# Graph attention over edges: scores as two full-array matmuls on block keys, and keys copied one item ahead

## The chip, the core and the metric

The kernel runs on one core of a Trainium2 chip. The metric is the device time of one execution in microseconds (us). The kernel before was run three times: 1605.08, 1602.91 and 1599.86 us, median 1602.91. The trace and the profile's page below come from one further execution, taken by the hardware profiler.

## The reference, cut to what matters

A graph of 6250 nodes with 256 features has 106,250 edges. After a layer norm, each node sends its row to its neighbours with attention weights, and the result is added to the input. A mixture-of-experts layer (8 experts, top 2) follows; the change does not touch it.

```
q = tanh(x @ Wq + bq)                     # 6250 x 25
k = x @ Wk + bk                           # 6250 x 25
w = sum(q[src] * k[dst]) / 5              # one score per edge
alpha = softmax of w over the edges of one dst
out = segment_sum(alpha * x[src], dst)    # 6250 x 256
x = x + out
x = x + moe(layernorm(x))                 # top-2 of 8 experts, 256 -> 512 -> 256
```

## The kernel before, in words

There are three stages. The first normalises the rows, computes q and k and writes a table of rows (256 features, a one, 25 values of q) to memory. The second is the edge loop. The third runs the experts.

The edge loop handles 106 items. An item has two halves (called x), each a group of 512 edges (four sub-groups j of 128) and a window of 64 target nodes. So 128 partitions hold the nodes of both halves. For an item *a* the engines do this, each with its own written order:

- **GpSimd (POOL)** issues eight indirect gathers of 128 rows each into one of four slots of `xg` (`gather`, line 586). The gathers for item a wait until the sums of item a-4 are done (semaphore `s_pv`).
- **ScalarE (ACT)** runs `item` (lines 1409 to 1416): it copies q out of the slot once the gathers have landed (line 1392), takes the exponentials of item a-1 (lines 1401 and 1402), copies the keys of item a (four copies, one for each 32 nodes, line 1386), copies the transposed q (line 1397), and copies the transposed probabilities of item a-1 (line 1407).
- **TensorE (PE)** runs `item` (lines 1660 to 1666): two transposes of q (line 1631), four transposes of the probabilities of a-1 (line 1647), the scores of a (line 1640), the weighted sums of a-1 (line 1655). The scores are eight matmuls with 25 rows, 64 columns of weights and 128 moving columns, for two halves and four sub-groups, into four PSUM banks. The sums are eight matmuls with 64 columns of weights and 257 moving columns.
- **VectorE (DVE)** copies the running maxima (line 931), subtracts, masks and reduces the scores of item a (line 936), stores the maxima (line 943), makes the mask of item a+1 (line 921), and adds the sums of a-1 to the accumulator (line 954).

Four items form a `quad`; the loop over quads runs with values read from a table at run time, so the windows and groups are computed in registers (lines 322 and 332). Six times in the loop a chunk of 896 nodes is complete. In such a quad VectorE also normalises the finished rows (`finished`, lines 988 to 1013), and in the next one it sorts them to experts (`route`, lines 1048 to 1120); ScalarE and TensorE have their share in both. The SyncE queue loads indices and targets for each item; at the end of the loop it waits until the keys of the last item have been copied (semaphore `s_kts`) and then issues the loads of the first experts' weights (lines 474, 475 and 480), which overwrite the keys' memory.

Of the kernel before, what the change touches and what calls it, by code (L numbers as in the profile page):

```python
# [28 lines left out]
P = 128  # L29
N = 6250  # L30
D = 256
S = 25
# [13 lines left out]
HP = P // 2  # L46
# [7 lines left out]
G = 4  # L54
# [5 lines left out]
BAND = P // G  # L60
ROW = D + 1 + S
W1COLS = D + 1
# [15 lines left out]
DK = 5.0  # L78
# [18 lines left out]
def build(nc, x, src, dst, Wq, bq, Wk, bk, gamma, beta, Wr, br, W1, b1, W2, b2, out):  # L97
    ctx = ExitStack()
    with ctx:
        def sb(name, shape, dt=F32):  # L100
            return ctx.enter_context(nc.sbuf_tensor(name, shape, dt))
# [17 lines left out]
        ident = sb("ident", [P, P])  # L119
# [7 lines left out]
        wqk = sb("wqk", [P, 2, 2 * S])  # L127
        bqk = sb("bqk", [P, 2 * S])
        bkcol = sb("bkcol", [P, 1])
# [27 lines left out]
        done_i = arena_b[0:1, 9788:9789].bitcast(I32)  # L157
        done_b = arena_b[0:1, 9789:9789 + NE]
        gidx_e = arena_b[:, 9797:9797 + 2 * EARLY].bitcast(I32)


        arena_a = sb("arena_a", [P, 12712])
        qz = arena_a[:, 0:NT * S].rearrange("p (t s) -> p t s", t=NT)
        rawf = arena_a[:, 1300:1300 + 1024]
# [58 lines left out]
        idx = sb("idx", [P, XSLOTS, 2, G], I32)  # L223
        kts = sb("kts", [P, P])
        qs = sb("qs", [P, 2, G, BAND])
        qT = sb("qT", [P, 2, P])
# [31 lines left out]
        wsel = sb("wsel", [P, 2])  # L258
        weq = sb("weq", [P, 2])
        wtok = sb("wtok", [P, 2])  # L260
        tokB = sb("tokB", [P, 2], I32)
        b1e = sb("b1e", [P, 4])
        gidx = sb("gidx", [P, 2], I32)
# [3 lines left out]

        score_banks = ps[:, 4 * 512:8 * 512].rearrange("p (j n) -> p j n", j=G)[:, :, 0:P]
        sums_bank = [pb[3], pb[1]]
# [407 lines left out]
        def _(v):  # L677
# [17 lines left out]
            v.memset(ltok[:, :], 0.0).then_inc(s_v0, 1)  # L695
            v.memset(kT[:, NT * P:NTX * P], 0.0).then_inc(s_v0, 1)
            v.sem_inc(s_acc, 2)
            v.sem_inc(s_mask, PEEL)
# [75 lines left out]
            def group_lists():  # L774

                v.wait_ge(s_grpb, 1)
                for b in range(2):
                    v.tensor_copy(cntb[:, 2 * b:2 * b + 2, :].rearrange("p k (q h) -> p k h q", h=2),
                                  pb[6 + b][:, 0:4 * GP].rearrange("p (k h q) -> p k h q", k=2, h=2)).then_inc(s_grpd, 1)
                v.wait_ge(s_v0, 16)  # L780
                v.wait_ge(s_grpd, 10)
# [105 lines left out]
            v.wait_ge(s_kc, 1)  # L887
            v.wait_ge(s_v0, 16)
            v.tensor_copy(segf[:, 0:NCH - 1], pb[7][0:1, 0:NCH - 1]).then_inc(s_sg, 1)
# [35 lines left out]
            def maximum(b, tiles, a, number, first=False):  # L925

                if not first:
                    v.wait_ge(s_ms, number(a))
                    v.sem_inc(tk_v, 1)
                for r in range(4):  # L930
                    ins = v.tensor_copy(nmo[quarters[r], b:b + 1], nm_all[quarters[r], bass.ds(tiles(r // 2, a)[r % 2], 1)])  # L931
                ins.then_inc(s_om, 1)
                v.wait_ge(s_om, number(a + 1))
                v.wait_ge(s_sc, number(a + 1))
                v.sem_inc(tk_v, 1)
                v.tensor_tensor_reduce(out=sc[:, b, :].rearrange("p (j n) -> p j n", j=G), in0=score_banks[:, :, :],  # L936
                                       in1=mask[:, b, :].rearrange("p (j n) -> p j n", j=G), scale=-1.0 / DK,
                                       scalar=nmo[:, b:b + 1], op0=ALU.add, op1=ALU.min,
                                       accum_out=nbias[:, b:b + 1]).then_inc(s_nb, 1)
                v.wait_ge(s_nb, number(a + 1))  # L940
                v.sem_inc(tk_v, 1)
                for r in range(4):
                    ins = v.tensor_copy(nm_all[quarters[r], bass.ds(tiles(r // 2, a)[r % 2], 1)], nbias[quarters[r], b:b + 1])  # L943
                ins.then_inc(s_ms, 1)
# [335 lines left out]
        def _(a):  # L1280
# [5 lines left out]
            for o, i in ((bqk[:, 0:S], bq.partition_broadcast(P)),  # L1286
# [5 lines left out]
                a.dma_start(o, i).then_inc(s_wl, 16)  # L1292
            a.wait_ge(s_v0, 16)
            for j in range(G):
# [87 lines left out]

            def copy_keys_of(tiles, a_):
                for r in range(4):
                    cols = slice(r * BLK, (r + 1) * BLK)
                    ins = nc.scalar.copy(kts[:, cols], kT3[:, bass.ds(tiles(r // 2, a_)[r % 2], 1), cols].rearrange("p o n -> p (o n)"))
                ins.then_inc(s_kts, 1)

            def copy_q(s, landed):
                a.wait_ge(s_g[s], landed)  # L1390
                a.sem_inc(tk_a, 1)
                nc.scalar.copy(qs[:, :, :, 0:S], xg[:, s * 2 * G:(s + 1) * 2 * G, W1COLS:ROW]  # L1392
                               .rearrange("p (x j) d -> p x j d", x=2)).then_inc(s_qs, 1)
# [11 lines left out]
            def copy_probs(b, done):  # L1405
                a.wait_ge(s_pt, done)
                nc.scalar.copy(probT[:, b, :], pb[2][:, :]).then_inc(s_pts, 1)

            def item(tiles, a_, number, landed, between=None):
                copy_q(a_ % XSLOTS, landed)  # L1410
                exponentials((a_ - 1) % 2, number(a_))
                copy_keys_of(tiles, a_)
                copy_qT(number(a_ + 1))
                copy_probs((a_ - 1) % 2, number(a_))
                if between is not None:
                    between()

            number = counter(a, 0)
            copy_keys_of(tiles, 0)
            copy_q(0, 32 * G)  # L1420
            copy_qT(1)
            item(tiles, 1, number, 32 * G)
            def quad(k, ends=None, routes=None):

# [123 lines left out]
        def _(pe):  # L1548
# [79 lines left out]
            def q_transposes(done):  # L1628
                pe.wait_ge(s_qs, done)
                for x_ in range(2):  # L1630
                    last = nc.tensor.transpose(pb[0][:, x_ * P:(x_ + 1) * P], qs[:, x_, :, :].rearrange("p j s -> p (j s)"), ident[:, :])  # L1631
                last.then_inc(s_qt, 1)

            def scores(done):
                pe.wait_ge(s_kts, done)
                pe.wait_ge(s_qTs, done)
                for x_ in range(2):
                    for j in range(G):
                        band = slice(j * BAND, j * BAND + S)
                        last = mm(score_banks[HP * x_:HP * x_ + HP, j, :], kts[band, HP * x_:HP * x_ + HP], qT[band, x_, :],  # L1640
                                  start=True, stop=True)
                last.then_inc(s_sc, 1)
# [17 lines left out]
            def item(a, number, between=None):  # L1660
                q_transposes(number(a + 1))
                prob_transposes((a - 1) % 2, number(a))
                scores(number(a + 1))
                sums((a - 1) % 2, (a - 1) % XSLOTS, number(a), number(a))
                if between is not None:
                    between()
# [8 lines left out]
            q_transposes(1)  # L1675
            scores(1)
            item(1, number)
# [170 lines left out]
```

## Time and profile before

| | |
|---|---|
| median of three runs | 1602.91 us |
| profiled execution, span from first to last instruction | 1973.1 us |
| edge loop in the profiled execution, first to last gather | 94.36 to 1538.11 us |
| TensorE busy | 57% of the span |
| GpSimd busy | 56% |
| VectorE busy | 43% |
| ScalarE busy | 25% |
| granted TensorE clock, mean over the span | 0.700 |

The page gives no other time for the profiled execution than its span, and the span is 370 us longer than the median of the runs. Busy shares are means over stages of very different kind: the first stage, the edge loop and the experts. A time at the start of a row of the timeline is counted from the first instruction, the next number is how long the work took, and the square brackets say how long the engine had been idle and who ended it.

### The profile page before, as it was taken

The numbers are of one execution on the slowest core, as the hardware profiler recorded it, in microseconds if no ns is written. First come the engines' busy times: TensorE is split into PE (matmuls) and PEld (weight loads), VectorE is DVE, ScalarE is ACT, GpSimd is POOL, SyncE is SP. The second block draws the span as 40 slices with busy tenths as digits, with TensorE's granted clock in tenths as the row PEclk, the third lists the DMA queues.
The fourth block names the chain that finished last, engine by engine and source line by source line (L and its number), as shares of the span: only waits on it lengthen the run. The fifth ranks groups of instructions, "written<-read, shape, count | busy, mean of one in ns | idle before, by whom it ended". The sixth has DMA issues, their size and how long they took to land.

```text
span 1973.1 us, 30781 instructions
## 1 busy us (share of the span) xinstructions
PE 1132.6 (57%) x6718; PEld 766.9 (39%) x6719; DVE 840.2 (43%) x3273; ACT 499.6 (25%) x1477; POOL 1114.7 (56%) x1111
## 2 busy tenths in 40 slices
PE   6623444444445445455354445454454789999997
PEld 6511222322223223122232223122231568888886
DVE  7513343454344534444345334444445653333332
ACT  3511122121212122122121222122121433443342
POOL 3255666464665565646644664646654357677676
PEclk9756666565656556666565666666565799999999
DMA  8554434344333534533435333534345435554554
GB/s 185 135 114 106 107 101 104 105 112 107 103 104 106 128 102 111 127 97 102 105 88 123 101 102 94 130 93 105 101 112 125 131 72 95 91 106 81 94 94 64
DMA packets 155658, 210.22 MB, mean 107 GB/s; under 512 B 59526, under 2 KB 122462, under 8 KB 155431
## 3 DMA queue, kind: packets, MB, share of 16 engines
q0 software_dynamic: 61360, 151.84, 32.4%
q1 hardware_dynamic: 74921, 40.52, 8.6%
q10 hardware_dynamic: 19278, 16.96, 3.6%
q14 instruction: 87, 0.70, 0.1%
q8 instruction: 12, 0.20, 0.0%
HBM read 174.36 MB, written 34.41 MB: 106 GB/s over the span
## 4 chain that ended last, share of the span: by engine, by line
PE 23%; issue 23%; DVE 19%; another core or an unknown queue 16%; DVEq 12%; SPq 2%; ACT 2%; ACTq 1%; DMA 1%; POOL 0%; POOLq 0%
PE pb L1766 8%; PE pb L1775 8%; DVEq L332 5%; DVE acc L954 3%; DVE arena_b L936 3%; DVEq L322 3%; DVE nmo L931 2%; DVE nm_all L943 2%; PE pb L1756 1%; PE pb L1655 1%; PE pb L1707 1%; DVE ab L1111 1%; DVEq L954 1%; DVE mask L921 1%
## 5 line engine op out<-in xcount | busy, mean ns | idle before, releaser
L586 POOL DMA_INDIRECT arena_a<-rows_dram,idx x848 | 813.8, 960 | 652.4 <-issue 240.2
L1655 PE MATMUL pb<-arena_a,arena_b 128*64 128x257 f32 x1696 | 358.1, 596 | 8.1 <-issue 4.5
L954 DVE SCALAR_TENSOR_TENSOR acc<-acc,alpha,pb 32x257 f32 x424 | 203.4, 480 | 319.8 <-issue 175.8
L1640 PE MATMUL pb<-qT,kts 25*64 25x128 f32 x1696 | 75.6, 425 | 340.8 <-ACT qT L1397 331.7
L1647 PE MATMUL pb<-ident,arena_b 128*128 128x128 f32 x424 | 94.7, 363 | 251.5 <-ACT arena_b L1401 158.9
L1655 PEld LDWEIGHTS pb<-arena_a,arena_b 128*64 128x64 f32 x1696 | 171.7, 211 | 155.8 <-issue 119.1
L1401 ACT ACTIVATE arena_b<-arena_b,nbias 128x512 f32<-128x512 f32 x106 | 76.4, 721 | 549.4 <-DVE nbias L936 407.5
L1766 PE MATMUL pb<-arena_a,arena_b 128*128 128x256 f32 x832 | 192.0, 384 | 1.2 <-ACT arena_a L1503 1.2
L630 POOL DMA_INDIRECT out_dram<-arena_a,tokB x104 | 166.1, 1597 | 45.2 <-issue 26.0
L1775 PE MATMUL pb<-arena_b,arena_a 128*128 128x256 f32 x832 | 188.3, 379 | 0.6 <-DVE arena_a L1177 0.6
L1640 PEld LDWEIGHTS pb<-qT,kts 25*64 25x64 f32 x1696 | 37.3, 192 | 370.6 <-issue 346.6
L1647 PEld LDWEIGHTS pb<-ident,arena_b 128*128 128x128 f32 x424 | 64.5, 186 | 277.9 <-ACT arena_b L1401 174.9
L1766 PEld LDWEIGHTS pb<-arena_a,arena_b 128*128 128x128 f32 x832 | 159.9, 193 | 23.9 <-issue 1.4
L1775 PEld LDWEIGHTS pb<-arena_b,arena_a 128*128 128x128 f32 x832 | 154.1, 190 | 19.7 <-DVE arena_a L1177 0.9
L1514 ACT ACTIVATE arena_a<-pb,b1e 128x256 f32<-128x256 f32 x208 | 98.7, 474 | 220.5 <-PE pb L1766 191.3
L936 DVE CUSTOM_DVE_ANT_0 arena_b<-pb,mask,nmo 128x512 f32<-128x512 f32 x106 | 79.6, 751 | 175.1 <-remote 119.7
L609 POOL DMA_INDIRECT arena_a<-xn_dram,gidx x100 | 99.7, 997 | 65.3 <-PE pb L1756 45.0
L1177 DVE TENSOR_TENSOR arena_a<-pb,arena_b 128x256 f32<-128x256 f32 x104 | 43.9, 424 | 203.5 <-PE pb L1775 108.1
L921 DVE TENSOR_SCALAR mask<-arena_b,win_node 64x512 bf16<-64x512 int16 x214 | 79.1, 369 | 87.8 <-issue 79.1
L1397 ACT COPY qT<-pb 128x256 f32<-128x256 f32 x106 | 39.1, 369 | 279.2 <-remote 273.7
L931 DVE COPY nmo<-nm_all 32x1 f32 x424 | 61.4, 145 | 101.8 <-issue 95.2
L1631 PE MATMUL pb<-ident,qs 128*128 128x128 f32 x212 | 60.4, 378 | 45.9 <-ACT qs L1392 25.6
(236 smaller groups left out, 1231.2 us busy)
## 6 DMA issues: line engine op xcount, KB each, us to landing
arena_a<-rows_dram,idx POOLq DMA_INDIRECT x848
arena_b<-dst_dram SPq DMA_DIRECT2D x210, 64.0 KB
arena_b<-in_L_ffn_W_dram SPq DMA_DIRECT2D x16, 512.0 KB
rows_dram<-acc SPq DMA_DIRECT2D x12, 493.5 KB, 5.5
acc<-in_x_dram SPq DMA_DIRECT2D x13, 448.0 KB, 15.6
xn_dram<-arena_a ACTq DMA_DIRECT2D x6, 910.0 KB
out_dram<-arena_a ACTq DMA_DIRECT2D x12, 448.0 KB
idx<-srccol SPq DMA_DIRECT2D x214, 2.0 KB
```

The costliest lines, as they stand in the source:

```text
L586: g.indirect_dma_start(out=xg[:, (s * 2 + x_) * G + j, :], out_offset=None, in_=rows_dram[:, :], in_offset=bass.IndirectOffsetOnAxis(ap=id ...
L609: g.indirect_dma_start(out=xrows[:, k, :], out_offset=None, in_=xn_dram[0:rows_there, :], in_offset=bass.IndirectOffsetOnAxis(ap=columns[: ...
L630: g.indirect_dma_start(out=out[:, :], in_=ybuf[:, k, :], in_offset=None, out_offset=bass.IndirectOffsetOnAxis(ap=tokB[:, k:k + 1], axis=0) ...
L921: ins = v.tensor_scalar(mask[rows_of, b, :], dstb[rows_of, s, :], win_node[rows_of, bass.ds(window(x_, a), 1)], -BIG, ALU.not_equal, ALU.mult)
L931: ins = v.tensor_copy(nmo[quarters[r], b:b + 1], nm_all[quarters[r], bass.ds(tiles(r // 2, a)[r % 2], 1)])
L936: v.tensor_tensor_reduce(out=sc[:, b, :].rearrange("p (j n) -> p j n", j=G), in0=score_banks[:, :, :], in1=mask[:, b, :].rearrange("p (j n ...
L954: ins = v.scalar_tensor_tensor(out=mine, in0=mine, scalar=alpha[rows_of, b:b + 1], in1=sums_bank[b][rows_of, 0:W1COLS], op0=ALU.mult, op1= ...
L1640: last = mm(score_banks[HP * x_:HP * x_ + HP, j, :], kts[band, HP * x_:HP * x_ + HP], qT[band, x_, :], start=True, stop=True)
L1647: last = nc.tensor.transpose(pb[2][:, j * P:(j + 1) * P], sc[:, b, j * P:(j + 1) * P], ident[:, :])
L1655: last = mm(sums_bank[b][HP * x_:HP * x_ + HP, 0:W1COLS], probT[:, b, j * P + HP * x_:j * P + HP * x_ + HP], xg[:, (s * 2 + x_) * G + j, 0 ...
L1766: last = mm(banks[m][:, 0:ST], w1s[:, b, c, m * P:(m + 1) * P], xT[:, c, :], start=c == 0, stop=c == 1, skip_group_check=True)
L1775: last = mm(pb[3 + k2][:, 0:D], hT[:, c, k2 * P:(k2 + 1) * P], w2s[:, b, c, :], start=c == 0, stop=c == 3)
```

## The change

Line 1640's eight matmuls become two. The q of sub-groups 2h and 2h+1 of both halves are laid side by side before the transposes, so that one transposed tile has its 128 partitions filled with (sub-group parity o, half, feature). The keys are laid as blocks: for each parity o, the 64 columns of a half are non-zero only in the partitions of that half. One matmul for each o, 128 rows, 128 columns of weights and 256 moving columns, then gives the scores of two sub-groups for both halves. All scores now lie in one PSUM bank. The block keys take eight copies of 32 partitions by 32 columns in place of four of 128 by 32; they have two buffers, zeroed once at the start, and the keys of item a+1 are copied at the end of ScalarE's item a. VectorE's reduction reads one bank of 512 values in place of four pieces of 128. Some small tiles move into other memory, with no other instructions.

```diff
-        kts = sb("kts", [P, P])
-        qs = sb("qs", [P, 2, G, BAND])
+        kts = sb("kts", [P, 2, 2, P])
+        qs = sb("qs", [P, G, 2, BAND])
...
-        score_banks = ps[:, 4 * 512:8 * 512].rearrange("p (j n) -> p j n", j=G)[:, :, 0:P]
+        score_bank = pb[4]
+        score_pairs = score_bank[:, :].rearrange("p (h o n) -> p o h n", h=2, o=2)
...
+            v.memset(kts[:, :, :, :], 0.0).then_inc(s_v0, 1)
...
-                v.tensor_tensor_reduce(out=sc[:, b, :].rearrange("p (j n) -> p j n", j=G), in0=score_banks[:, :, :],
-                                       in1=mask[:, b, :].rearrange("p (j n) -> p j n", j=G), scale=-1.0 / DK,
+                v.tensor_tensor_reduce(out=sc[:, b, :], in0=score_bank[:, :], in1=mask[:, b, :], scale=-1.0 / DK,
...
-            def copy_keys_of(tiles, a_):
+            def copy_keys_of(b, tiles, a_):
                 for r in range(4):
                     cols = slice(r * BLK, (r + 1) * BLK)
-                    ins = nc.scalar.copy(kts[:, cols], kT3[:, bass.ds(tiles(r // 2, a_)[r % 2], 1), cols].rearrange("p o n -> p (o n)"))
+                    for o in range(2):
+                        band = slice((2 * o + r // 2) * BAND, (2 * o + r // 2 + 1) * BAND)
+                        ins = nc.scalar.copy(kts[band, b, o, cols],
+                                             kT3[band, bass.ds(tiles(r // 2, a_)[r % 2], 1), cols].rearrange("p o n -> p (o n)"))
                 ins.then_inc(s_kts, 1)
...
                 exponentials((a_ - 1) % 2, number(a_))
-                copy_keys_of(tiles, a_)
                 copy_qT(number(a_ + 1))
                 copy_probs((a_ - 1) % 2, number(a_))
+                copy_keys_of((a_ + 1) % 2, tiles, a_ + 1)
...
-            def scores(done):
+            def scores(b, done):
                 pe.wait_ge(s_kts, done)
                 pe.wait_ge(s_qTs, done)
-                for x_ in range(2):
-                    for j in range(G):
-                        band = slice(j * BAND, j * BAND + S)
-                        last = mm(score_banks[HP * x_:HP * x_ + HP, j, :], kts[band, HP * x_:HP * x_ + HP], qT[band, x_, :],
-                                  start=True, stop=True)
+                for o in range(2):
+                    last = mm(score_pairs[:, o, :, :], kts[:, b, o, :], qT[:, :, :], start=True, stop=True)
                 last.then_inc(s_sc, 1)
```

On ScalarE, in the second item of a quad, this stood from the exponentials to the transposed q (`kts` are the copied keys, `arena_b` holds the keys of all nodes, `qT` is the transposed q):

```order
L1402 ACTIVATE alpha<-nmo,nbias 128x1
L322 REGISTER_ALU x2
L322 ISA
L1386 COPY kts<-arena_b 128x32
L1386 ISA
...
L1397 COPY qT<-pb 128x256 [waits s_qt]
L1407 COPY arena_b<-pb 128x512 [waits s_pt]
L1437 REGISTER_ALU
L1392 COPY qs<-arena_a 128x8x25 [waits s_g0]
```

And this stands there now; the item's table word for the next keys is read here as well (`TENSOR_LOAD`):

```order
L1406 ACTIVATE alpha<-nmo,nbias 128x1
L370 REGISTER_ALU
L1401 COPY qT<-pb 128x256 [waits s_qt]
L1411 COPY arena_b<-pb 128x512 [waits s_pt]
L333 ISA
L333 TENSOR_LOAD item_row
L333 ISA x2
L323 REGISTER_ALU
L323 ISA
L1389 COPY kts<-arena_b 32x32
```

The copies of keys have moved from before the transposed q to behind the transposed probabilities, ahead of the wait for the next gathers.

On TensorE, the stretch of one item before was:

```order
L1631 MATMUL pb<-ident,qs 128x128 [waits s_qs]
L1631 MATMUL pb<-ident,qs 128x128
L1647 MATMUL pb<-ident,arena_b 128x128 [waits s_p]
L1647 MATMUL pb<-ident,arena_b 128x128 x3
L1640 MATMUL pb<-qT,kts 64x128 [waits s_qTs,s_kts]
L1640 MATMUL pb<-qT,kts 64x128 x7
L1655 MATMUL pb<-arena_a,arena_b 64x257 [waits s_acc,s_pts]
L1655 MATMUL pb<-arena_a,arena_b 64x257 x7
```

and is now, in the same place:

```order
L1650 MATMUL pb<-ident,arena_b 128x128 x3
L1644 MATMUL pb<-qT,kts 128x2x128 [waits s_qTs,s_kts]
L1644 MATMUL pb<-qT,kts 128x2x128
L1658 MATMUL pb<-arena_a,arena_b 64x257 [waits s_acc,s_pts]
L1658 MATMUL pb<-arena_a,arena_b 64x257 x7
```

The order of the steps is the same; eight matmuls of 64 by 128 columns have become two of 128 by 256.

## Rows read from the trace of the kernel before

**Rows 1.** The page: span, busy times, and the TensorE clock over 40 slices.

```profile
span 1973.1 us, 30781 instructions
PE 1132.6 (57%) x6718; PEld 766.9 (39%) x6719; DVE 840.2 (43%) x3273; ACT 499.6 (25%) x1477; POOL 1114.7 (56%) x1111
PEclk9756666565656556666565666666565799999999
```

**Rows 2.** By stretch: length; PE, PEld, DVE, ACT, POOL busy; clock; DMA share; GB/s.

```profile
0.00:110.00 110.00, 65.93 (x384) 59.18 (x385) 68.30 (x265) 44.01 (x119) 36.94 (x61) 0.84 0.71 158
110.00:1550.00 1440.00, 664.21 (x4374) 359.56 (x4374) 613.83 (x2298) 294.12 (x1017) 804.97 (x840) 0.61 0.42 107
1550.00:1973.00 423.00, 402.44 (x1960) 348.18 (x1960) 158.07 (x711) 161.50 (x341) 272.81 (x211) 0.98 0.48 92
```

**Rows 3.** The page's costliest groups: gathers.

```profile
L586 POOL DMA_INDIRECT arena_a<-rows_dram,idx x848 | 813.8, 960 | 652.4 <-issue 240.2
```

**Rows 4.** Timeline of GpSimd: the first gather of the loop, and the last.

```profile
94.36 1.07 POOL L586 DMA_INDIRECT arena_a<-rows_dram,idx  x1 [21.57 <-DMA rows_dram<-acc]
...
1538.11 0.96 POOL L586 DMA_INDIRECT arena_a<-rows_dram,idx  x1 [0.30 <-issue]
```

**Rows 5.** Timeline of all engines around one ordinary item.

```profile
616.19 1.96 PE L1655 MATMUL pb<-arena_a,arena_b 128*64 128x257 f32 x16
...
618.08 0.44 PE L1631 MATMUL pb<-ident,qs 128*128 128x128 f32 x2
...
622.29 1.11 PE L1647 MATMUL pb<-ident,arena_b 128*128 128x128 f32 x4 [3.77 <-ACT arena_b L1401]
...
625.11 0.37 ACT L1397 COPY qT<-pb 128x256 f32<-128x256 f32 x1 [1.35 <-remote]
...
625.26 1.96 DVE L954 SCALAR_TENSOR_TENSOR acc<-acc,alpha,pb 32x257 f32 x4 [1.25 <-remote]
...
625.82 0.96 POOL L586 DMA_INDIRECT arena_a<-rows_dram,idx  x1 [2.59 <-remote]
...
630.46 0.56 ACT L1386 COPY kts<-arena_b 128x32 f32 x4
...
638.10 0.95 POOL L586 DMA_INDIRECT arena_a<-rows_dram,idx  x1 [2.46 <-remote]
```

**Rows 6.** Timeline after a finished chunk: the first two items, and GpSimd.

```profile
386.85 0.37 ACT L1392 COPY qs<-arena_a 128x200 f32<-128x200 f32 x1 [1.53 <-issue]
...
390.74 0.34 ACT L1386 COPY kts<-arena_b 128x32 f32 x2 [1.39 <-issue]
...
391.50 0.74 PE L1640 MATMUL pb<-qT,kts 25*64 25x128 f32 x16 [2.44 <-ACT qT L1397]
...
392.16 3.70 PE L1655 MATMUL pb<-arena_a,arena_b 128*64 128x257 f32 x16
...
396.66 0.95 POOL L586 DMA_INDIRECT arena_a<-rows_dram,idx  x1 [14.00 <-PE pb L1655]
...
397.03 0.48 PE L1640 MATMUL pb<-qT,kts 25*64 25x128 f32 x16
```

**Rows 7.** VectorE's busy time while it finishes one chunk and sorts another.

```profile
585.06:600.00 14.94, 9.17 (x34) 0.50 0.40 103
...
651.97:676.10 24.13, 13.36 (x73) 0.50 0.74 173
```

**Rows 8.** The chain that ended last: transfers and matmuls after the loop.

```profile
1547.82 7.09 DMA arena_a<-xn_dram,arena_b
...
1592.56 2.81 DMA arena_a<-xn_dram,arena_b
...
1951.67 3.46 PE pb L1775 x16
```

**Rows 9.** Timeline of VectorE at the start: a memset, and the first statistics.

```profile
4.92 0.40 DVE L695 MEMSET ltok<- 128x408 f32 x1
...
8.96 2.38 DVE L706 BATCH_NORM_STATS2 st<-acc 128x6 f32<-128x256 f32 x7 [3.50 <-DMA acc<-in_x_dram]
```

More of the change, by code:

```diff
@@ L127, in build @@
         wqk = sb("wqk", [P, 2, 2 * S])
-        bqk = sb("bqk", [P, 2 * S])
         bkcol = sb("bkcol", [P, 1])
@@ L158, in build @@
         done_b = arena_b[0:1, 9789:9789 + NE]
+        b1e = arena_b[:, 9806:9810]
+        weq = arena_b[:, 9810:9812]
+        wtok = arena_b[:, 9812:9814]
         gidx_e = arena_b[:, 9797:9797 + 2 * EARLY].bitcast(I32)
         arena_a = sb("arena_a", [P, 12712])
+        bqk = arena_a[:, 9024:9024 + 2 * S]
         qz = arena_a[:, 0:NT * S].rearrange("p (t s) -> p t s", t=NT)
@@ L258, in build @@
         wsel = sb("wsel", [P, 2])
-        weq = sb("weq", [P, 2])
-        wtok = sb("wtok", [P, 2])
         tokB = sb("tokB", [P, 2], I32)
-        b1e = sb("b1e", [P, 4])
         gidx = sb("gidx", [P, 2], I32)
@@ L779, in group_lists @@
                                   pb[6 + b][:, 0:4 * GP].rearrange("p (k h q) -> p k h q", k=2, h=2)).then_inc(s_grpd, 1)
-                v.wait_ge(s_v0, 16)
+                v.wait_ge(s_v0, 17)
                 v.wait_ge(s_grpd, 10)
@@ L887, in _ @@
             v.wait_ge(s_kc, 1)
-            v.wait_ge(s_v0, 16)
+            v.wait_ge(s_v0, 17)
             v.tensor_copy(segf[:, 0:NCH - 1], pb[7][0:1, 0:NCH - 1]).then_inc(s_sg, 1)
@@ L1292, in _ @@
                 a.dma_start(o, i).then_inc(s_wl, 16)
-            a.wait_ge(s_v0, 16)
+            a.wait_ge(s_v0, 17)
             for j in range(G):
@@ L1391, in copy_q @@
                 a.sem_inc(tk_a, 1)
-                nc.scalar.copy(qs[:, :, :, 0:S], xg[:, s * 2 * G:(s + 1) * 2 * G, W1COLS:ROW]
+                nc.scalar.copy(qs[:, :, :, 0:S].rearrange("p j x d -> p x j d"), xg[:, s * 2 * G:(s + 1) * 2 * G, W1COLS:ROW]
                                .rearrange("p (x j) d -> p x j d", x=2)).then_inc(s_qs, 1)
@@ L1418, in _ @@
             number = counter(a, 0)
-            copy_keys_of(tiles, 0)
+            copy_keys_of(0, tiles, 0)
             copy_q(0, 32 * G)
             copy_qT(1)
+            copy_keys_of(1, tiles, 1)
             item(tiles, 1, number, 32 * G)
@@ L1629, in q_transposes @@
                 pe.wait_ge(s_qs, done)
-                for x_ in range(2):
-                    last = nc.tensor.transpose(pb[0][:, x_ * P:(x_ + 1) * P], qs[:, x_, :, :].rearrange("p j s -> p (j s)"), ident[:, :])
+                for h in range(2):
+                    last = nc.tensor.transpose(pb[0][:, h * P:(h + 1) * P],
+                                               qs[:, 2 * h:2 * h + 2, :, :].rearrange("p j x s -> p (j x s)"), ident[:, :])
                 last.then_inc(s_qt, 1)
-            def scores(done):
+            def scores(b, done):
                 pe.wait_ge(s_kts, done)
                 pe.wait_ge(s_qTs, done)
-                for x_ in range(2):
-                    for j in range(G):
-                        band = slice(j * BAND, j * BAND + S)
-                        last = mm(score_banks[HP * x_:HP * x_ + HP, j, :], kts[band, HP * x_:HP * x_ + HP], qT[band, x_, :],
-                                  start=True, stop=True)
+                for o in range(2):
+                    last = mm(score_pairs[:, o, :, :], kts[:, b, o, :], qT[:, :, :], start=True, stop=True)
                 last.then_inc(s_sc, 1)
@@ L1662, in item @@
                 prob_transposes((a - 1) % 2, number(a))
-                scores(number(a + 1))
+                scores(a % 2, number(a + 1))
                 sums((a - 1) % 2, (a - 1) % XSLOTS, number(a), number(a))
@@ L1675, in _ @@
             q_transposes(1)
-            scores(1)
+            scores(0, 1)
             item(1, number)
```

## The prediction

> **What bounds the kernel now.** I began with the page's span, busy shares and clock [rows 1]. No engine is busy for more than 57% of the span, and the clock row shows three stages: near full speed at both ends, 5 to 6 tenths between. Busy time by stretch [rows 2] gives them: 110 us of first stage, some 1440 us of edge loop, and 423 us in which TensorE is busy for 402 us at a clock of 0.98. The change touches the loop, so the question is what sets the pace there.
>
> The profiled span is 1973.1 us and the median of the runs 1602.9, so the profiled execution lost 370 us that the runs don't lose. I have to find where before I use any duration. TensorE and VectorE are busy for less than half of the loop, but GpSimd for 805 of 1440 us. Its work is 848 gathers of 960 ns [rows 3], and each has 0.30 us of idle time in front of it in which it waits for nothing that is shown [rows 4]. That is 1.26 us a gather and 10.1 us for the eight of an item. 848 x 1.26 = 1068.5 us. The loop's gathers go from 94.36 to 1539.07, which is 1444.7 us [rows 4]. So GpSimd paused for 376 us in all. Take these pauses out of the span and 1597 us are left: 6 us from the median of the runs, or 0.4%. The sum that fits the runs is therefore a loop in which the gathers are issued with hardly a pause.
>
> What the pauses are, the timeline of an ordinary item shows [rows 5]. GpSimd's gathers of successive items start at 625.82 and 638.10, 12.3 us apart, with 2.5 us of pause ended by "remote". At 616.19 TensorE begins the sums, for which 1.96 us are modelled; yet VectorE, which adds them, gets going at 625.26. The two transposes of q are recorded at 618.08 with 0.44 us, but the copy of their result starts at 625.11. So for one item TensorE's results reach the others about 7 us after the modelled end, and two that can't end together (0.44 us of transposes behind the sums) arrive within 0.2 us. Where GpSimd stands still, the lag is absent: the sums of 392.16 take 3.70 us, end at 395.86, and the waiting gather starts at 396.66 [rows 6]. I read the lag as mostly due to the recording of many small TensorE instructions while gathers run, since the runs without the profiler can't hold it in full. That it is wholly absent there is my choice, not shown.
>
> **The change part by part.** *TensorE's scores.* Eight matmuls go, two of 256 moving columns come. The nearest row is an expert matmul, 128 x 128 by 256: sixteen records (two for each matmul) in 3.46 us at full clock [rows 8], so 0.43 us each and 0.86 us for two. Before it was 0.48 us at the full clock and 0.74 at the half one [rows 6]. The sums stretch from 1.96 [rows 5] to 3.70 us [rows 6], by 1.89, so at the half clock two take 1.6 us. The scores lengthen by 0.4 us (full) to 0.9 us (half, which the loop mostly has). Beside a 10.1 us stream of gathers this is hidden. TensorE's item at the half clock is 0.7 of transposed q, 1.1 of transposed probabilities, 0.7 of scores and 3.7 of sums, 6.2 us, and becomes 7.1. Its cover is the 3 us left.
>
> The row is 0.48 us for eight matmuls that, one after the other at half of 0.43 us each, would take 1.7: they do overlap. The Trainium skill (TensorEngine Tiling (Array Packing), Theoretical Speedup) speaks against the change here: it promises up to 4x for a contraction of at most 32 and 2x for 64 columns, and both are given up. By it the new scores would be up to four times 0.48 us, an estimate of 1.9 at full clock, against 0.86 by the row; under the gathers both cost nothing. The same page (Tiling Modes, Key Properties) says that changing the tiling mode drains the engine, and the change removes one of three shapes per item; no row here prices it.
>
> *ScalarE's key copies.* Four took 0.56 us [rows 5]; eight take about 1.1, with their address registers. ScalarE is busy for 294 us in the loop, 2.8 an item [rows 2], and would be at 3.4 of 10.1. They stand now where ScalarE waits for the next gathers, so the item that follows gets its transposed q sooner. What that is worth shows after a chunk: q is copied at 386.85, the keys only by 391.08 (the table word is read there too), and the scores wait 2.44 us and start at 391.50; the sums end at 395.86 [rows 6]. Without the keys the scores start when the transposed probabilities are done, about 2.2 us after 386.85 (1.1 us of them, rows 5, behind the q transposes): 389.1. With 1.6 us of scores the sums run from 390.8 to 394.5, 1.4 us earlier. In an item without the table read the keys cost only 0.56 us, less than the 0.9 by which the scores grow, so there the sums come up to 0.3 us later. Late next, in both, is the gather.
>
> *VectorE's reduction* has the same 512 values, from one bank. The bound is nothing on either side of its unchanged element count; I take 0.
>
> *The zeroing of the keys* is one memset of 512 values; 408 took 0.40 us [rows 9], so 0.5 us, and VectorE then waits 3.50 us for the input [rows 9]. It costs nothing; uncovered it would be 0.5 us.
>
> *The end of the loop.* SyncE starts the weight loads when the last item's keys are copied. That now happens at the end of the item before, some 7 us sooner, while that last item's gathers are still being issued. The loads' traffic is what a gather meets after the loop: 7.09 us to land just behind the loads, against 2.81 later [rows 8]. So the last gather may land up to 4.3 us later; in exchange the expert gathers meet less traffic, but they are not what ends last there by more than a us. Bounds: 0 to +4.3. I take +2, as only part of the gathers overlap.
>
> *Do the chunks stall GpSimd without the profiler?* Gathers for item a+4 start some 28 us after q of a has been copied and need its sums, which end one item (10.1) and 9.0 us later [rows 6]: 9 us of slack. VectorE has 613.8 us of work in the loop, of which two stretches a chunk with 9.2 and 13.4 us busy, 135 in six chunks [rows 2, 7]; so 4.5 us an item, and 5.6 free. Sorting holds it for 24.1 us, finishing for 14.9 [rows 7]. Over its free time that is 18.5 and 9.3 us, over the slack about 10 and 0. Six such pauses would be 60 us, and 1597 + 60 is above the runs. So either part of these stretches is lag as well, or a gather is issued a little faster than 1.26 us (0.07 us would do it). If they exist, the change gains up to 1.4 us at the first item after each. I take half of 6 x 1.4, 4 us, as gain.
>
> The sum, against the profiled execution freed of its pauses: 1597 - 4 + 2 = 1595; set on the median of the runs, 1602.9 - 2 = 1601. I say 1600.
>
> **Rivals.** *Faster.* (a) GpSimd does pause at both stretches of every chunk and the keys are what holds the next sums: 12 x 1.4 = 17 us, 1586. For it: 14.0 us of pause ended by TensorE's sums [rows 6]. Against: the sum fits without. (b) The lag of TensorE is partly real in the runs too and goes with the number of its small matmuls. Then the gathers are issued faster than 1.26 us and the loop is paced by TensorE. If one half us an item went, 53 us: 1550. Against: the closeness of 1597 to 1602.9 would be chance.
>
> *Slower.* After a pause the four slots are full and the next items run at TensorE's pace, not GpSimd's. With a half clock each first sum comes 0.9 us later, as the item there turns out not to wait for keys: 12 exits x 0.9 = 11 us, and with 4.3 us from the weight loads 1618. It decides as soon as GpSimd waits for sums at more than five exits. For it: clock 0.61 in the loop [rows 2]; against: the 2.44 us wait at the keys [rows 6].
>
> *The change doesn't do what it says*: the copies for the next item sit ahead of the wait for gathers, so they can't delay them; if ScalarE still came late, it would be at the table reads, and the time would be as before, 1603. That is in the first case.
>
> **How the numbers follow.** About 0.3%, 5 us, is what a measurement of this kernel can tell from no change. The forecast, no change within it: 0.46, 1600 us, own range 1596 to 1607. Faster 0.34 (0.26 for (a), 0.08 for (b)). Slower 0.20. The range goes to the slower rival's near end, 1612, and past (a)'s 1586 to 1582, which leaves out most of (b) and the slower rival's tail.
>
> **What would show it.** In the profile of the changed kernel: gathers of 0.96 us with 0.30 us ahead, unchanged; scores in 4 records of 0.8 us at full clock; key copies x848 behind the transposed probabilities, and no wait of TensorE on them; in an ordinary item TensorE's lag and GpSimd's 2.5 us pause smaller, since an item has 12 matmul records fewer (4 in place of 16); so the profiled span should fall well below 1973 while the runs don't. The prediction is wrong if the runs move with the profiled span, or if gathers take another time, or if the pauses stay with fewer records.

## The result, and the profile after

The changed kernel took 1609.97 us (median of nine runs, 1604.83 to 1612.34); the kernel before, run beside it, 1604.65 us (nine runs, 1599.13 to 1606.54). The ratio is 1.004, interval 1.0026 to 1.0053: slower by about 5 us. The prediction said no change at 1600 us.

One fact has to be known first, since the numbers can't be read without it: the kernel before takes about 1602 us on some chips and 1974 us on others. Of four chips that were used for the experiments two gave medians of 1974.06 and 1973.69 us (29 and 20 runs), two 1600.69 and 1602.88 us (29 and 19 runs). By its span of 1973.1 us the profile of before came from the second kind; its timed runs and this profile of the changed kernel came from the first. Below they are called the 1602 us chip and the 1974 us chip, and kernels are compared only on the same one. The kernel before as it stands was not profiled on a 1602 us chip; there its variant with early loads, which comes below, stands in for it.

The page of the changed kernel has its span, busy times and the TensorE clock, to be read beside [rows 1]:

```profile
span 1604.7 us, 29319 instructions
PE 1144.0 (71%) x5446; PEld 815.9 (51%) x5447; DVE 837.1 (52%) x3274; ACT 626.4 (39%) x1909; POOL 1112.3 (69%) x1111
PEclk9998766687777778787777877777788999999999
```

By stretch (length; PE, PEld, DVE, ACT, POOL busy; clock; DMA share; GB/s), beside [rows 2]:

```profile
0.00:110.00 110.00, 75.64 (x366) 71.71 (x367) 68.07 (x266) 44.67 (x121) 32.09 (x57) 1.00 0.70 155
110.00:1180.00 1070.00, 661.70 (x3102) 393.58 (x3103) 611.38 (x2297) 418.56 (x1439) 807.54 (x844) 0.75 0.57 147
1180.00:1604.00 424.00, 406.63 (x1979) 350.59 (x1978) 157.69 (x711) 163.20 (x350) 272.68 (x211) 0.97 0.47 86
```

The loop shrank from about 1440 to 1070 us. The busy times in it stayed within 1%, but for ScalarE's (294 to 419 us) and TensorE's weight loads (360 to 394 us), which belong to the change. It is the pauses that are missing, not work. The groups on the page (busy us, mean ns of one, idle time before and what ended it), beside [rows 3]:

```profile
L587 POOL DMA_INDIRECT arena_a<-rows_dram,idx x848 | 813.0, 959 | 281.3 <-issue 247.8
...
L1389 ACT COPY kts<-arena_b 32x32 f32 x856 | 184.1, 215 | 68.3 <-issue 60.6
...
L1644 PE MATMUL pb<-qT,kts 128*128 128x256 f32 x424 | 187.6, 592 | 0.6 <-ACT qT L1401 0.6
```

The gathers are as predicted, 0.96 us with 0.30 ahead of each (281.3 us of idle for 848, of which 23 precede the first). They run from 99.03 to 1169.21 us, and no two start more than 1.45 us apart. TensorE waits for keys nowhere. Its results are used at once: an ordinary item of the changed kernel, in the timeline, beside [rows 5]:

```profile
628.05 1.92 PE L1644 MATMUL pb<-qT,kts 128*128 128x256 f32 x4
...
629.43 0.95 POOL L587 DMA_INDIRECT arena_a<-rows_dram,idx  x1 [0.30 <-issue]
629.89 2.00 PE L1658 MATMUL pb<-arena_a,arena_b 128*64 128x257 f32 x16
630.14 0.75 DVE L938 CUSTOM_DVE_ANT_0 arena_b<-pb,mask,nmo 128x512 f32<-128x512 f32 x1 [3.63 <-PE pb L1644]
...
630.68 0.96 POOL L587 DMA_INDIRECT arena_a<-rows_dram,idx  x1 [0.30 <-issue]
```

The scores end at 629.97, and VectorE, which had been waiting for them for 3.63 us, starts 0.17 us later; the 7 us between TensorE's modelled end and its readers in [rows 5] are absent.

The end of the loop shows where the 5 us are. In the timeline of the changed kernel:

```profile
1165.34 1.80 ACT L1389 COPY kts<-arena_b 32x32 f32 x8
...
1167.23 0.39 SPq L475 DMA_DIRECT2D arena_b<-in_L_ffn_W_dram  x1
1167.67 0.46 SPq L476 DMA_DIRECT2D arena_b<-in_L_ffn_W_dram  x1
1168.18 0.50 SPq L481 DMA_DIRECT2D arena_b<-in_L_ffn_b_dram  x1
1168.72 0.64 SPq L475 DMA_DIRECT2D arena_b<-in_L_ffn_W_dram  x1
...
1169.40 0.75 SPq L476 DMA_DIRECT2D arena_b<-in_L_ffn_W_dram  x1
...
1177.41 0.37 ACT L1396 COPY qs<-arena_a 128x200 f32<-128x200 f32 x1 [10.28 <-DMA arena_a<-rows_dram,idx]
```

The last item's keys are now copied at 1165.34 to 1167.14, and five loads follow while the last two gathers (1167.95 and 1169.21) are issued. q is copied at 1177.41, 7.25 us after the last gather's end at 1170.16. In the profile of before, the last gather ended at 1539.07 [rows 4], q was copied 3.1 us later, and the loads came behind it:

```profile
1542.21 0.37 ACT L1392 COPY qs<-arena_a 128x200 f32<-128x200 f32 x1 [0.51 <-DMA arena_a<-rows_dram,idx]
...
1546.09 0.39 SPq L474 DMA_DIRECT2D arena_b<-in_L_ffn_W_dram  x1
```

### The profile page after: what moved, and what is told of

It is laid out like the page before. It is cut to its first block, busy times and chain, and to the rows that moved or that the text cites. A ratio compares the mean times of both kernels' runs of the same rounds, so it can differ in the third digit from the quotient of the medians.

```text
span 1604.7 us, 29319 instructions
## 1 busy us (share of the span) xinstructions
PE 1144.0 (71%) x5446; PEld 815.9 (51%) x5447; DVE 837.1 (52%) x3274; ACT 626.4 (39%) x1909; POOL 1112.3 (69%) x1111
## 3 DMA queue, kind: packets, MB, share of 16 engines
q1 hardware_dynamic: 74921, 40.52, 10.6%
## 4 chain that ended last, share of the span: by engine, by line
PE 37%; POOL 30%; issue 17%; DMA 7%; DVE 5%; DVEq 1%; ACT 1%; SPq 1%; ACTq 0%; POOLq 0%
POOL arena_a L587 29%; PE pb L1778 10%; PE pb L1769 10%; DMA arena_a<-rows_dram,idx 5%; PE pb L1658 4%; PE pb L1644 3%; PE pb L1650 2%; PE pb L1584 2%; PE pb L1759 1%; PE pb L1636 1%; PE pb L1569 1%; DMA acc<-in_x_dram 1%; ACT qs L1396 1%; PE pb L1735 1%; PE pb L1710 0%
## 5 line engine op out<-in xcount | busy, mean ns | idle before, releaser
L587 POOL DMA_INDIRECT arena_a<-rows_dram,idx x848 | 813.0, 959 | 281.3 <-issue 247.8
L1658 PE MATMUL pb<-arena_a,arena_b 128*64 128x257 f32 x1696 | 264.2, 465 | 0.7 <-ACT arena_b L1411 0.7
L1636 PEld LDWEIGHTS pb<-ident,qs 128*128 128x128 f32 x212 | 26.9, 177 | 386.9 <-ACT qs L1396 385.3
L1396 ACT COPY qs<-arena_a 128x200 f32<-128x200 f32 x106 | 38.8, 366 | 456.3 <-DMA arena_a<-rows_dram,idx 424.9
L1389 ACT COPY kts<-arena_b 32x32 f32 x856 | 184.1, 215 | 68.3 <-issue 60.6
L1658 PEld LDWEIGHTS pb<-arena_a,arena_b 128*64 128x64 f32 x1696 | 138.7, 173 | 139.9 <-issue 102.3
L1644 PE MATMUL pb<-qT,kts 128*128 128x256 f32 x424 | 187.6, 592 | 0.6 <-ACT qT L1401 0.6
L1519 ACT ACTIVATE arena_a<-pb,arena_b 128x256 f32<-128x256 f32 x208 | 98.5, 474 | 219.4 <-PE pb L1769 219.3
L1650 PE MATMUL pb<-ident,arena_b 128*128 128x128 f32 x424 | 107.5, 402 | 46.9 <-ACT arena_b L1405 46.5
L1644 PEld LDWEIGHTS pb<-qT,kts 128*128 128x128 f32 x424 | 119.2, 309 | 19.5 <-issue 0.9
L1650 PEld LDWEIGHTS pb<-ident,arena_b 128*128 128x128 f32 x424 | 68.5, 199 | 79.1 <-ACT arena_b L1405 79.1
```

Of the source, the lines that this page charges most:

```text
L587: g.indirect_dma_start(out=xg[:, (s * 2 + x_) * G + j, :], out_offset=None, in_=rows_dram[:, :], in_offset=bass.IndirectOffsetOnAxis(ap=id ...
L1389: ins = nc.scalar.copy(kts[band, b, o, cols], kT3[band, bass.ds(tiles(r // 2, a_)[r % 2], 1), cols].rearrange("p o n -> p (o n)"))
L1519: nc.scalar.activation(hT[:, m, :], banks[m][:, 0:ST], ACT.Gelu, bias=b1e[:, m:m + 1]).then_inc(b_g, 1)
L1636: last = nc.tensor.transpose(pb[0][:, h * P:(h + 1) * P], qs[:, 2 * h:2 * h + 2, :, :].rearrange("p j x s -> p (j x s)"), ident[:, :])
L1644: last = mm(score_pairs[:, o, :, :], kts[:, b, o, :], qT[:, :, :], start=True, stop=True)
L1650: last = nc.tensor.transpose(pb[2][:, j * P:(j + 1) * P], sc[:, b, j * P:(j + 1) * P], ident[:, :])
```

## The experiments

Most kernels were run on one chip of each kind. Beside each time stands that of the kernel before on the same chip. Where an expectation was written before a 1974 us chip was met, it has the times of the other kind.

**The loads behind the last item again, and the keys alone.** In the changed kernel SyncE waits for q of the last item, as late as it was before:

```diff
-            sp.wait_ge(s_kts, n_items)
+            sp.wait_ge(s_qs, n_items)
```

> The changed kernel, but the loads of the experts' weights wait for the last item's copy of q (so for its gathers), as they in effect did before. Theory 1 (the weight loads, issued an item early, delay the last two gathers): the 4 us come back, 1605 us, ratio to before 0.999 to 1.001; the last gather is followed by the copy of q after 3 us, not 7. Theory 2 (the longer scores and the eight key copies cost time in the items): it stays at 1609 to 1610, ratio 1.003 to 1.004.

> The changed kernel with the weight loads waiting for the last item's q, a second time. Theory 1 (the early weight loads cost the 5 us where the loop runs without pauses): 1605 us there, ratio 0.999 to 1.001, and below the changed kernel by 4 us or more. Theory 2 (longer scores, key copies): equal to the changed kernel within 1 us.

On the 1602 us chip 1601.08 us against 1600.69 before: ratio 0.9999 (0.9985 to 1.0012). The changed kernel itself, on the same chip:

> The changed kernel, unchanged, on whichever chip this call gets. Where the kernel before takes 1603 to 1606 us: 1610 us, ratio 1.003 to 1.005. Where it takes 1974 us, TensorE's results come up to 7 us late in the loop and the gathers pause for TensorE; there the change should stand near the variant with late weight loads (1967 us), ratio 0.995 to 1.000, since the pace is set by TensorE's items and not by the last gather.

1606.08 us, ratio 1.0028 (1.0014 to 1.0042), a little under the expected 1.003. So 5.0 us go with the loads, and no loss is left that these runs could tell: theory 2 falls. With late loads the last gather and what follows it read:

```profile
1168.87 0.95 POOL L587 DMA_INDIRECT arena_a<-rows_dram,idx  x1 [0.30 <-issue]
...
1172.99 0.37 ACT L1396 COPY qs<-arena_a 128x200 f32<-128x200 f32 x1 [5.95 <-DMA arena_a<-rows_dram,idx]
...
1173.45 0.39 SPq L475 DMA_DIRECT2D arena_b<-in_L_ffn_W_dram  x1
```

q is copied 3.2 us after the gather's end; in the changed kernel on the same chip it is 7.6 us. On the 1974 us chip the late loads gave 1966.99 us against 1974.06, 0.9967 (0.994 to 0.9993). The changed kernel itself was not run there.

The other way round, in the kernel before SyncE waits only for the keys of the item before the last:

```diff
-            sp.wait_ge(s_kts, n_items)
+            sp.wait_ge(s_kts, kept(sp, n_quads * 4 + PEEL - 1, NG // 2 - 1, ITEMS))
```

> The kernel before, with one thing changed: the loads of the experts' weights wait for the keys of the last item but one. Theory 1: slower by 4 to 5 us, ratio 1.0025 to 1.003, and the copy of the last q comes 7 us after the last gather's issue. Theory 2: no change, ratio within 0.001 of 1.

> The kernel before with the weight loads an item early, a second time. Theory 1: slower by 4 to 5 us where the loop runs without pauses, ratio 1.0025 to 1.003. Theory 2: ratio within 0.001 of 1.

1604.78 us against 1600.69, ratio 1.0019 (1.0006 to 1.0032): early loads alone make the kernel before 4.1 us slower. On the 1974 us chip 1979.84 against 1974.06, 1.0013 (0.9989 to 1.0036), which tells nothing apart. It could not: in its profile there the first load is issued at 1552.30, 3.0 us after the last gather (1549.28), and q is copied 2.95 us after that gather's end, as with late loads.

**Part of the loads early.** In the changed kernel two loads go as early as they do and three wait:

```diff
             load_w(0, 0)
+            sp.wait_ge(s_qs, n_items)
             sp.dma_start(b2b[:, :, :].rearrange("p e d -> p (e d)"),
```

> The changed kernel in which SyncE issues the first expert's two weight loads as early as it does, and the other three loads only once the last item's q has been copied. Theory (the loads' traffic delays the last two gathers): part of the traffic is left, so between the kernel before and the changed one, +1.5 to +4 us over before. Rival (it is the first load alone that the gathers queue behind): the full +4 to +5 us. Rival (the loads of the second expert are what gets in the way): +0 to +1 us.

> The changed kernel with only the first expert's two weight loads early, run again because the first time it was measured where the kernel before itself takes 1974 us. If the kernel before takes about 1601 us here: traffic theory +1.5 to +4 us over it; first load alone +4 to +5 us; second expert's loads +0 to +1 us.

1604.46 us against 1602.88 (1602 us chip), ratio 1.001 (0.9997 to 1.0023): +1.6 us, between none and all. On the 1974 us chip it was 1966.02 against 1973.69, 0.9971 (0.9941 to 1.0001). By the time alone the first could be no change; the chain of waits (start, us, what) tells more. It holds the last gather's transfer in each kernel. Late loads, two early, and all five early:

```profile
1168.87 4.00 DMA arena_a<-rows_dram,idx
```

```profile
1168.03 5.73 DMA arena_a<-rows_dram,idx
```

```profile
1170.43 8.40 DMA arena_a<-rows_dram,idx
```

And five early in the kernel before:

```profile
1170.83 7.48 DMA arena_a<-rows_dram,idx
```

From the last gather's issue to its landing it takes 4.0 us with no weight load in flight, 5.7 with two, 7.5 to 8.4 with five (8.1 in the first profile of the changed kernel). In the changed kernel, run again, the DMA engines are 96% busy while it waits, with late loads 50% (by stretch, columns as above; 1170 to 1179 of the one, 1168 to 1173 of the other):

```profile
1170.00:1179.00 9.00, 0.00 (x0) 0.00 (x0) 5.13 (x19) 0.06 (x1) 4.23 (x6) 0.74 0.96 307
```

```profile
1168.00:1173.00 5.00, 0.00 (x0) 0.00 (x0) 4.42 (x16) 0.01 (x1) 4.09 (x6) 0.97 0.50 113
```

With two loads they are 97% busy, but only for the 5.7 us. The delay grows with the loads and the DMA engines are full: the theory of traffic holds. "Only the first load matters" falls, and so does "only the second expert's loads matter": two loads of the first give 1.7 of the 4.4 us.

**Keys back on the item's path.** The changed kernel copies its eight block keys within the item, ahead of the transposed q, and none for the next:

```diff
                 exponentials((a_ - 1) % 2, number(a_))
+                copy_keys_of(a_ % 2, tiles, a_)
                 copy_qT(number(a_ + 1))
                 copy_probs((a_ - 1) % 2, number(a_))
-                copy_keys_of((a_ + 1) % 2, tiles, a_ + 1)
...
-            copy_keys_of(1, tiles, 1)
```

> The changed kernel, but the eight key copies of an item stand where the four stood, ahead of the transposed q, and the weight loads again wait for the last item's keys. Theory 1: the loads are late again, so 1605 us, ratio 0.999 to 1.001, although scores and copies are the new ones. Theory 2, with the keys back on the path: at least as slow as the changed kernel, 1610 us or more, ratio 1.003 to 1.01.

> The changed kernel with the key copies back ahead of the transposed q, a second time. Where TensorE's results are late it cost 3.5% (2043 us). Where gathers set the pace, theory 1 expects 1605 us, ratio 0.999 to 1.001, since 10 us of gathers hide the items; theory 2 expects 1.003 or more.

On the 1602 us chip 1615.31 us against 1600.69, ratio 1.0093 (1.0076 to 1.011); on the 1974 us chip 2043.55 against 1974.06, 1.0349 (1.0311 to 1.0386). Theory 1, no loss, falls; theory 2's 1.003 to 1.01 holds on the 1602 us chip and is far exceeded on the other. The loads are late here as before, and with late loads the same scores and the same eight copies cost nothing with the copies at the item's end (1601.08 us). So the 14 us between the two are due to where the copies stand. The timeline on the 1602 us chip shows one of the places (the exit from a chunk that has been sorted):

```profile
534.46 1.79 ACT L1389 COPY kts<-arena_b 32x32 f32 x8
...
536.27 0.37 ACT L1401 COPY qT<-pb 128x256 f32<-128x256 f32 x1
...
536.79 2.05 PE L1643 MATMUL pb<-qT,kts 128*128 128x256 f32 x4 [1.25 <-ACT qT L1401]
...
538.76 2.58 PE L1657 MATMUL pb<-arena_a,arena_b 128*64 128x257 f32 x16
...
538.91 0.95 POOL L587 DMA_INDIRECT arena_a<-rows_dram,idx  x1 [0.30 <-issue]
...
542.15 0.95 POOL L587 DMA_INDIRECT arena_a<-rows_dram,idx  x1 [2.29 <-PE pb L1657]
```

The same item in the kernel before (with early loads, same chip):

```profile
537.28 0.56 ACT L1386 COPY kts<-arena_b 128x32 f32 x4
...
538.29 0.73 PE L1640 MATMUL pb<-qT,kts 25*64 25x128 f32 x16
...
539.03 3.35 PE L1655 MATMUL pb<-arena_a,arena_b 128*64 128x257 f32 x16
...
543.60 0.95 POOL L586 DMA_INDIRECT arena_a<-rows_dram,idx  x1 [0.30 <-issue]
```

There the sums end at 542.38, and the gather that needs them could go at 543.60 + 0.95 + 0.30 = 544.85: 2.5 us to spare. With eight copies of 1.79 us (in place of 0.56) and scores of 2.05 us (in place of 0.73) on the path the spare is gone and GpSimd stands still. I worked this spare time out for all items, from the modelled end of an item's sums to the end of the gather ahead of the waiting one plus 0.30:

| on the 1602 us chip | spare, median | spare at the six exits from a sorted chunk | first to last gather |
|---|---|---|---|
| before, loads early | 11.4 us | 2.1 to 2.8 us | 1071.0 us |
| changed | 11.9 us | 1.7 to 3.7 us | 1070.2 us |
| changed, scores three times, loads late | 10.6 us | -1.1 to +0.3 us | 1079.8 us |
| changed, keys in the item | 9.4 us | -2.3 to -1.0 us | 1085.4 us |

**The scores three times.** `for o in range(2)` became `for o in (0, 1) * 3` in the changed kernel with late loads; the same result is written again.

> The changed kernel with the weight loads back behind the last item's gathers, and each of the two score matmuls issued three times (the same result is written again). The page has 1.77 us of scores an item (187.6 us over 106), so four more add 3.5 us to TensorE's 6.2 us an item, 9.8 us in all against 10.1 us of gathers. Theory A (gathers set the pace, and what TensorE does beside them costs only where the slack is used up, after a finished chunk): an ordinary item stays at 10.1 us and six exits from a chunk lose up to 3.5 us each and its echo in the items after, +10 to +30 us over the kernel before. Rival B (scores lie on the path of each item): 106 x 3.5 = +370 us. Rival C (all is hidden, at the chunks too): within 3 us of the kernel before.

> The changed kernel with late weight loads and each score matmul three times, run again. Where the kernel before takes 1974 us it gave 1990. If the kernel before takes about 1601 us here: theory A (gathers cover an ordinary item, the exits from six chunks don't) 1611 to 1631 us; rival C (all hidden) 1598 to 1604; rival B (on the path of each item) about 1970.

On the 1602 us chip 1609.51 us against 1602.88, ratio 1.0049 (1.0029 to 1.0068), +6.6 us; on the 1974 us chip 1989.89 against 1973.69, 1.0079 (1.0048 to 1.011). Four more matmuls an item, 215 us of TensorE by the page's busy times (402.8 in place of 187.6 us, 1272 records in place of 424), cost 7 us. GpSimd's pauses sum to 7.2 us, and 6.4 of them are at the six exits from sorted chunks. The time is a little under the lower end of theory A's range (1611 us); being on every item's path falls.

**Half of the gathers.** Of each item's eight gathers only four are issued, in both kernels; the other half of the rows is left out (in the changed kernel with the loads late):

```diff
-                    for j in range(G):
+                    for j in range(0, G, 2):
```

> The changed kernel with the weight loads late, and with only four of an item's eight gathers issued, the other half of the rows left out (their slots are zeroed once). It shows what an item costs when gathers don't cover it. Gathers would take 4 x 1.26 = 5.0 us an item. Theory A (gathers set the pace): the loop falls from 1070 us to TensorE's pace, some 6.5 to 8 us an item, 690 to 850 us, total about 1220 to 1390 us; and against the same cut in the kernel before it is slower by the longer scores, 0.5 to 1.1 us an item, +50 to +115 us. Rival (the key copies ahead take more off the path than the scores add): faster than the same cut of before by up to 50 us. Rival (something other than gathers sets the pace of the loop): both cuts leave the time above 1550 us.

> The kernel before with only four of an item's eight gathers issued, the other half of the rows left out (their slots are zeroed once). Theory A: 1170 to 1330 us, 50 to 115 us below the same cut of the changed kernel. Rival: above that cut by up to 50 us. Rival (gathers don't set the pace): above 1550 us.

> The changed kernel with late weight loads and half of an item's gathers left out, run again. Where the kernel before takes 1974 us it gave 1476, against 1514 for the same cut of before, and TensorE's results came 0.6 us late (median of the sums) in place of 7.4. If that lateness is a matter of the chip alone, the two kernels come closer to each other's 1070 us loops where it is absent: theory A 1350 to 1450 us. Rival (the cut is bound by something with no lag in it): 1470 again.

> The kernel before with half of an item's gathers left out, run again. 1514 us where the uncut kernel takes 1974. If its eight small score matmuls hold it up only by the lateness of their results (2.3 us median there), it equals the changed kernel's cut within 10 us here; if the keys on its path do, it stays 20 to 40 us above it.

On the 1602 us chip 1404.14 us (changed) and 1403.92 us (before): equal, and 199 us below the whole kernel's 1602.88. The gathers do set the pace of the whole kernel; of the cut ones something else does, since their loops still take 8.1 us an item and four gathers 5.0. On the 1974 us chip 1475.82 (changed) against 1513.57 (before): the change is worth 38 us there. Both are above the 1220 to 1390 and 1170 to 1330 us that I expected, and my +50 to +115 us for the longer scores missed on both chips; the 1350 to 1450 us for the 1602 us chip, and the equality of the two kernels there, came. What differs between the chips is how late TensorE's results are seen. Before, half of the gathers, on the 1974 us chip:

```profile
644.58 0.48 PE L1646 MATMUL pb<-qT,kts 25*64 25x128 f32 x16
...
646.77 0.96 POOL L592 DMA_INDIRECT arena_a<-rows_dram,idx  x1 [0.30 <-issue]
...
648.03 0.95 POOL L592 DMA_INDIRECT arena_a<-rows_dram,idx  x1 [0.30 <-issue]
...
650.22 0.75 DVE L942 CUSTOM_DVE_ANT_0 arena_b<-pb,mask,nmo 128x512 f32<-128x512 f32 x1 [3.32 <-remote]
```

And on the 1602 us chip:

```profile
709.58 0.60 PE L1646 MATMUL pb<-qT,kts 25*64 25x128 f32 x16 [1.23 <-ACT qT L1403]
...
712.69 0.31 DVE L937 COPY nmo<-nm_all 32x1 f32 x2 [0.86 <-issue]
713.22 0.75 DVE L942 CUSTOM_DVE_ANT_0 arena_b<-pb,mask,nmo 128x512 f32<-128x512 f32 x1 [0.22 <-DVE nmo L937]
```

In the first the scores end at 645.06 and VectorE, ready at 646.90, reads them at 650.22, 1.2 us after the last of GpSimd's four gathers has ended; in the second they are there when VectorE is ready. In 106 items another engine keeps VectorE waiting longer than 0.5 us ahead of this reduction 28 times in the first profile, twice in the second, and once in the changed kernel's cut on the 1974 us chip. That this makes up the 38 us is argued, not shown: no run there changes the lateness alone.

**The kernel before, unchanged.**

> The kernel before, unchanged, for a second profile. If the 376 us of pauses in its first profile come from recording its many small matmuls, the span is near 1970 us again while the runs stay at 1605; if they were an accident of that execution, the span is near 1600 us.

1974.58 us against 1974.06, ratio 1.0007 (0.9983 to 1.0032), span 1972.8 us: the pauses and the lateness of [rows 5] came back, and the runs without the profiler are as long. Neither branch of the expectation foresaw that.

## Why the prediction was wrong

**What bounds the kernel.** Right in its core: 848 gathers of 1.26 us set the pace of the loop (1070.2 us measured, 1068.5 worked out), and taking the pauses out of the profiled span led to the runs' time. The step "mostly due to the recording of many small TensorE instructions" fell: on two chips the same kernel takes 1974 us unrecorded, and its profile there has the same pauses. With it falls what I hung on it; the profiled span did fall by 370 us as foretold, but because the profile came from another kind of chip, not for the twelve records fewer an item. On a 1974 us chip the changed kernel with two early loads still takes 1431.3 us from its first to its last gather, where before takes 1441.1.

**Two terms of the sum failed.** It had -4 us for the keys and +2 for the end of the loop, so -2, where the runs show 0 and +4 to +5. The first missed by 4 us and the second by 2 to 3; neither alone would have brought the forecast to the measured +5.3 us. That 1609.97 lies within the range of 1582 to 1612 is luck: the upper part of it was there for stalls at the exits from chunks, which did not come, and my own range ended at 1607.

**The keys ahead**, "4 us, as gain", were worth nothing in this kernel: 1601.08 against 1600.69 us with the loads late. An earlier sum is worth something only where GpSimd waits for sums, and it does so nowhere: with the keys still in the item (the kernel before with early loads) 2.1 to 2.8 us are to spare at the tightest places. But the 15 us of the run with the eight copies in the item show that they had to be moved: the block layout needs this move to come out even.

**The end of the loop.** The mechanism was as put: the loads start an item early and slow the last gathers. Its size was not: "I take +2, as only part of the gathers overlap", with +4.3 as the upper bound. Measured are +4.1 us (loads early in the kernel before; 1.0 to 5.1 by its interval) and 5.0 us (loads early against late in the changed one); in the traces of one 1602 us chip the last gather lands 3.5 to 4.4 us later. The overlap was the wrong measure: all that counts is the very last gather, and that one is issued right among the loads. The return, less traffic for the expert gathers, isn't seen: after q of the last item 425.9 to 427.9 us pass with all five loads early (three profiles on 1602 us chips) and 425.4 to 429.9 with all late (three).

**Scores and keys** I priced too low. Scores went from 0.73 to 1.92 us at the half clock, +1.2 where I had +0.9, and from 0.48 to 1.10 at the full one, +0.6 where I had +0.4 (0.71 to 1.77 us an item over the loop: 75.1 us on the page of the kernel before with early loads, 187.6 on that of the changed one). Eight key copies take 1.80 us in a row, 1.74 us busy an item, not "about 1.1". I had taken each at the 0.14 us that the four took on average. But those overlap: a copy of 128 x 32 takes 211 ns and the next starts 107 to 125 ns after it, while one of 32 x 32 takes 215 ns and the next starts only when it has ended, 223 to 231 ns after it. Both are hidden, as I said, so the sum did not suffer.

**Do the chunks stall GpSimd?** I left it open, with pauses of 10 us by my own slack of 9 us. The median spare is 11.4 us and at the exits 2.1 us are left. My stretches of 24.1 and 14.9 us were read on the 1974 us chip.

**The rivals.** Faster (a) asked for GpSimd's pauses at the chunks and (b) for real lateness of TensorE: neither exists on the 1602 us chip. For the other kind of chip (b) had the direction, not the size: the change with late loads gained 7 us of 1974 there (0.33%), and 38 us once half of the gathers were gone. The slower rival had 4.3 us from the weight loads in it, which came, and 11 us from the exits, which did not. The corrected sum is 1602.9 + 4 to 5 = 1607 to 1608 us, against 1609.97 measured. Taken against the kernel before that was run beside it (1604.65 us) it is 1609 to 1610.

## What to carry to other kernels

A prefetch started earlier is not free when the last small transfers of the stage before are still on their way: look at what the final transfer meets, not at how many overlap. Where one engine's issue rate sets the pace, work out first how much time is to spare at the tightest place. If some is left, a saving on another engine gains nothing, and an addition costs only what goes beyond it. And a profiled span that stands far from the timed runs may come from another chip: no mechanism should be built on it before the same kernel has been timed where it was profiled.

## What the runs showed of the hardware

- On some chips TensorE's results reach the other engines late while GpSimd issues gathers. From the modelled end of an item's sums to the event that they raise it is 7.4 us (median of 106, kernel before) on the 1974 us chip and 0.03 us on the 1602 us chip (kernel before with early loads). With half of the gathers left out of the kernel before it is 0.03 us on both; for the small scores it is then 2.3 and 0.07 us, on the 1974 us chip as much as with all gathers (2.3). So the gather stream takes part in the lateness of the sums. Why only some chips have it stays open, and so does whether it stays with a chip: each of the four was seen only once.
- A gather of 128 rows takes the same 0.96 + 0.30 us on both kinds of chip: the median distance of two is 1.258 to 1.261 us in every profile of a whole kernel.
- ScalarE copies of 128 x 32 values start 107 to 125 ns apart and overlap (211 ns each); copies of 32 x 32 take 215 ns each and start 223 to 231 ns apart, one after the other. Four of the first took 0.56 us, eight of the second 1.80. What keeps the small ones from overlapping was not tried.
- The first gather started between 93.4 and 100.4 us in the profiles of whole kernels, which hardly differ up to there; single spans can't be compared to better than that.
